# Gate logits from un-normalised rows, the last rows normalised by ACT, and the first expert's slots loaded in two halves

## The reference

```
h = layernorm(x) * (1 + ca) + sa
x = x + ga * attention(h)                # 16 heads of 16, causal
h = layernorm(x) * (1 + cb) + sb
logits = h @ gate_weight.T               # 8 experts
probs = softmax(logits); top = argmax(logits)
rank of a token = how many earlier tokens chose the same expert; kept if rank < 320
y = probs[top] * gelu(h @ wi[top]) @ wo[top]      # kept tokens only, exact gelu
x = x + gb * y
```

## Time and profile before

| what | value |
|---|---|
| runs | 784.5, 790.14, 792.09 us |
| median | 790.14 us |
| span of the profiled execution | 782.6 us |
| time of the profiled execution | not given apart from its span |
| PE busy | 689.1 us, 88% |
| DVE busy | 561.1 us, 72% |
| ACT busy | 459.5 us, 59% |
| POOL busy | 133.9 us, 17% |
| mean granted clock of TensorE | 0.943 |
| DMA | 66.53 MB, 85 GB/s over the span |

### The profile page before, as it was taken

How to read it: one execution, slowest core, us unless ns; L and a number is a source line. 1 busy time by engine, 2 the same in 40 slices (tenths; PEclk the granted TensorE clock), 3 DMA queues, 4 the chain that set the end, 5 groups by cost and what they waited for, 6 DMA issues and landing times.

```text
span 782.6 us, 12208 instructions
## 1 busy us (share of the span) xinstructions
PE 689.1 (88%) x4290; PEld 367.2 (47%) x4290; DVE 561.1 (72%) x1467; ACT 459.5 (59%) x962; POOL 133.9 (17%) x194
## 2 busy tenths in 40 slices
PE   4686989999999998999999999989996279999994
PEld 3564534432323343323332323242543269999994
DVE  7754778788888787988888898960435437777762
ACT  1422445566676667766677676657783336656551
POOL 6000222220001132003310201100105300121122
PEclk9869889999999999999999999999999559999998
DMA  7436126630006033005900006000004283455200
GB/s 243 109 76 144 41 57 147 162 68 14 2 0 162 1 81 81 2 1 124 308 1 1 1 1 214 1 28 1 28 28 162 90 234 115 155 182 201 92 23 17
DMA packets 42111, 66.53 MB, mean 85 GB/s; under 512 B 3822, under 2 KB 31985, under 8 KB 41466
## 3 DMA queue, kind: packets, MB, share of 16 engines
q1 hardware_dynamic: 39746, 59.44, 27.3%
q0 software_dynamic: 2304, 6.31, 2.2%
HBM read 39.36 MB, written 26.78 MB: 85 GB/s over the span
## 4 chain that ended last, share of the span: by engine, by line
PE 74%; DVE 10%; ACT 8%; issue 4%; DMA 2%; POOL 1%; SPq 0%; DVEq 0%; POOLq 0%; ACTq 0%
PE bank L1245 17%; PE bank L1295 15%; PE bank L1325 14%; PE bank L1430 9%; PE bank L1413 8%; ACT probs L802 4%; PE bank L1187 3%; DVE chunk_max L1049 2%; PE bank L1350 2%; PE bank L1216 1%; PE bank L1396 1%; ACT qk_sb L751 1%; PE bank L1373 1%; PE bank L1228 1%; DVE stats L907 1%
## 5 line engine op out<-in xcount | busy, mean ns | idle before, releaser
L802 ACT ACTIVATE probs<-bank 128x512 f32<-128x512 f32 (+3 forms) x640 | 298.3, 537 | 124.1 <-PE bank L1325 123.0
L1049 DVE TENSOR_REDUCE chunk_max<-bank 128x1 f32<-128x512 f32 x384 | 250.7, 685 | 36.9 <-PE bank L1295 35.9
L1325 PE MATMUL bank<-stacks 104*128 104x512 bf16 (+3 forms) x640 | 195.4, 356 | 13.5 <-ACT probs L802 10.1
L1295 PE MATMUL bank<-stacks 96*128 96x512 bf16 (+3 forms) x640 | 197.7, 359 | 7.9 <-DVE chunk_max L1049 3.2
L1245 PE MATMUL bank<-probs,v_sb 128*32 128x512 f32 (+3 forms) x1280 | 151.6, 546 | 0.1
L1055 DVE CUSTOM_DVE_ANT_0 masked<-bank,causal 128x128 bf16<-128x128 f32 (+3 forms) x256 | 120.7, 484 | 15.4 <-PE bank L1295 14.6
L1295 PEld LDWEIGHTS bank<-stacks 96*128 96x128 bf16 x640 | 56.0, 98 | 160.0 <-DVE chunk_max L1049 79.4
L698 POOL TENSOR_SCALAR_AFFINE_SELECT probs<-probs 128x512 f32<-128x512 f32 x64 | 40.6, 635 | 397.4 <-ACT probs L802 397.4
L1325 PEld LDWEIGHTS bank<-stacks 104*128 104x128 bf16 x640 | 62.2, 100 | 98.7 <-ACT probs L802 65.6
L1430 PE MATMUL bank<-w_split,acts 128*128 128x256 f32 x576 | 79.9, 284 | 0.0
L1430 PEld LDWEIGHTS bank<-w_split,acts 128*128 128x128 f32 x576 | 74.5, 190 | 1.5 <-issue 0.8
(11 more groups left out here) (140 smaller groups left out, 533.6 us busy)
## 6 DMA issues: line engine op xcount, KB each, us to landing
stacks<-qk_rows SPq DMA_DIRECT2D x6, 1536.0 KB, 12.4
w_raw<-w_in SPq DMA_DIRECT2D x8, 1024.0 KB, 5.0
w_raw<-w_down SPq DMA_DIRECT2D x8, 1024.0 KB, 8.0
qk_rows<-part SPq DMA_DIRECT2D x32, 192.0 KB, 2.9
slot_rows<-empty SPq DMA_DIRECT2D x1, 5140.0 KB, 28.9
slots_sb<-slot_rows SPq DMA_DIRECT2D x8, 514.0 KB, 4.0
qk_rows<-part SPq DMA_DIRECT2D x32, 128.0 KB, 2.4
stacks<-qk_rows SPq DMA_DIRECT2D x8, 384.0 KB, 4.5
```

Of the source, the lines that this page charges most:

```text
L802: act.activation(probs[:, s % 3, h, 0:width], bank[SCORE_BANKS[u % 3]][:, 0:width], ACT.Exp)\
L1049: dve.tensor_reduce(to, src[:, 0:QB], AX.X, ALU.max).then_inc(max_read, 1)
L1295: pe.matmul(bank[MAX_BANKS[u % 3]][:, 0:width], stack(g, 0)[0:KR, h, q0:q0 + P], stack(g, 1)[0:KR, h, c * QB:c * QB + width], start=True, ...
L1325: pe.matmul(bank[SCORE_BANKS[u % 3]][:, 0:QB - lo], stack(g, 1)[0:KR + MR, h, kt * P:(kt + 1) * P], stack(g, 0)[0:KR + MR, h, b * QB + lo: ...
```

## The change

The gate's logits are formed from the turned x1 itself. With r the inverse root of a row's variance and m its mean, the normalised row times the scaled gate weights w' is r * (x1 @ w' - m * sum(w')), and that is r * (x1 @ (w' - column mean of w')). So the weights are centred once, at `gate_bias`: a second product with the scale's column in `product[:, 1]` puts the column sums of w' into columns E to 2E of the bank, and DVE subtracts them, divided by D, from the weights. `choose` multiplies by `rstd` and then adds the bias. `turn_normal` transposes `x_sb` and waits for `x1_ready`; the semaphore `xhat2_ready` is gone. The first 12 tiles are still normalised by DVE, for the scatter alone; the last four by ACT, behind the gate's exponential, with -mean * rstd as bias; POOL waits for each of them before its scatter. Expert 0's slots are loaded in two halves: columns 256 to 513 first, columns 0 to 255 behind the slots of experts 1 to 3; DVE waits for the second half in `add_rows`.

```diff
-        xhat2T = rest[:, :].rearrange("p (r n) -> p r n", r=2)
+        x1T = rest[:, :].rearrange("p (r n) -> p r n", r=2)
...
-        def load_slots(eng, e):
-            rows = slot_rows[e * CAP:(e + 1) * CAP, :]
-            eng.dma_start(slots_sb[:, e % SR, 0:CT3 - 1, :],
+        def load_slots(eng, e, cols=slice(0, ROW), done=None):
+            done = done or slots_loaded[e % SR]
+            rows = slot_rows[e * CAP:(e + 1) * CAP, cols]
+            eng.dma_start(slots_sb[:, e % SR, 0:CT3 - 1, cols],
...
             sp.wait_ge(scattered, 16 * NT)
-            for e in range(SR):
+            load_slots(sp, 0, slice(D, ROW), slots_first)
+            for e in range(1, SR):
                 load_slots(sp, e)
+            load_slots(sp, 0, slice(0, D))
...
                     for t in range(t0, t1):
+                        if t >= TAIL_TILES:
+                            pool.wait_ge(last_normal, t - TAIL_TILES + 1)
                         pool.indirect_dma_start(
...
                     act.activation(expd[:, t0:t1, :], expd[:, t0:t1, :], ACT.Exp).then_inc(exp_gate, 1)
+                    if t1 == NT:
+                        act.wait_ge(rstd_ready, 1)
+                        for i, t in enumerate(range(TAIL_TILES, NT)):
+                            act.activation(heads[:, t, :], x_sb[:, t, :], ACT.Identity, bias=shift_back[:, i:i + 1],
+                                           scale=rstd[:, t:t + 1]).then_inc(last_normal, 1)
...
-                    inverse_root(slice(t + 1 - TB, t + 1))
-                    for i in range(t + 1 - TB, t + 1):
-                        dve.tensor_scalar(heads[:, i, :], x_sb[:, i, :], mean_var[:, i, 0:1], rstd[:, i:i + 1],
-                                          ALU.subtract, ALU.mult).then_inc(xhat2_ready, 1)
+                    ts = slice(t + 1 - TB, t + 1)
+                    inverse_root(ts)
+                    if t < TAIL_TILES:
+                        for i in range(t + 1 - TB, t + 1):
+                            dve.tensor_scalar(heads[:, i, :], x_sb[:, i, :], mean_var[:, i, 0:1], rstd[:, i:i + 1],
+                                              ALU.subtract, ALU.mult)
+                    else:
+                        dve.scalar_tensor_tensor(out=shift_back[:, :], in0=mean_var[:, ts, 0], scalar=-1.0,
+                                                 in1=rstd[:, ts], op0=ALU.mult, op1=ALU.mult).then_inc(rstd_ready, 1)
...
-                                  bias, ALU.add).then_inc(logits_read, 1)
+                                  wide(rstd[:, ts]), ALU.mult).then_inc(logits_read, 1)
                 dve.wait_ge(logits_read, part_no + 1)
+                link(dve.tensor_tensor(logits[:, ts, :], logits[:, ts, :], bias, ALU.add))
...
-                    for ft in range(DT):
-                        shift = dve.tensor_scalar(product[:, 0, ft * P:(ft + 1) * P], ones_f[:, :],
-                                                  mod_col[:, 2, ft:ft + 1], None, ALU.mult)
-                    shift.then_inc(gate_rows_ready, 1)
+                    for m in range(2):
+                        for ft in range(DT):
+                            rows = dve.tensor_scalar(product[:, m, ft * P:(ft + 1) * P], ones_f[:, :],
+                                                     mod_col[:, 2 + m, ft:ft + 1], None, ALU.mult)
+                    rows.then_inc(gate_rows_ready, 1)
                     dve.wait_ge(misc_done, misc_use[ev] + 1)
-                    dve.tensor_copy(gate_bias[:, :], bank[MISC_BANK][:, 0:E]).then_inc(misc_read_v, 1)
                     for ft in range(DT):
                         scaled = dve.tensor_scalar(w_gate_sb[:, ft, :], w_gate_sb[:, ft, :], mod_col[:, 3, ft:ft + 1],
                                                    None, ALU.mult)
-                    scaled.then_inc(w_gate_ready, 1)
+                    link(scaled)
+                    for ft in range(DT):
+                        centred = dve.scalar_tensor_tensor(out=w_gate_sb[:, ft, :], in0=bank[MISC_BANK][:, E:2 * E],
+                                                           scalar=-1.0 / D, in1=w_gate_sb[:, ft, :], op0=ALU.mult,
+                                                           op1=ALU.add)
+                    centred.then_inc(w_gate_ready, 1)
+                    dve.tensor_copy(gate_bias[:, :], bank[MISC_BANK][:, 0:E]).then_inc(misc_read_v, 1)
...
             def add_rows(e, st):
+                if e == 0:
+                    dve.wait_ge(slots_loaded[0], 32)
...
-                    for k in range(DT):
-                        mm = pe.matmul(bank[MISC_BANK][:, 0:E], product[:, 0, k * P:(k + 1) * P], w_gate_sb[:, k, :],
-                                       start=(k == 0), stop=(k == DT - 1))
+                    for m in range(2):
+                        for k in range(DT):
+                            mm = pe.matmul(bank[MISC_BANK][:, m * E:(m + 1) * E], product[:, m, k * P:(k + 1) * P],
+                                           w_gate_sb[:, k, :], start=(k == 0), stop=(k == DT - 1))
...
-                    emptied(xhat2T_ready, t)
-                    pe.wait_ge(xhat2_ready, t + 1)
+                    emptied(x1T_ready, t)
+                    pe.wait_ge(x1_ready, t + 1)
                     for ft in range(DT):
-                        mm = pe.transpose(bank[tail_bank(2, t)][:, ft * P:(ft + 1) * P], heads[:, t, ft * P:(ft + 1) * P],
+                        mm = pe.transpose(bank[tail_bank(2, t)][:, ft * P:(ft + 1) * P], x_sb[:, t, ft * P:(ft + 1) * P],
...
             def turn_slots(e):
-                pe.wait_ge(slots_loaded[e % SR], 32 * (e // SR + 1))
+                if e == 0:
+                    pe.wait_ge(slots_first, 32)
+                else:
+                    pe.wait_ge(slots_loaded[e % SR], 32 * (e // SR + 1))
```

More of the change, by code:

```diff
@@ L321, in layer @@
         rstd = sb("rstd", [P, NT], F32)
+        shift_back = sb("shift_back", [P, TB], F32)
         product = sb("product", [P, 2, D], F32)
@@ L451, in layer @@
         x1_ready = sem("x1_ready")
-        xhat2_ready = sem("xhat2_ready")
-        xhat2_turned = sem("xhat2_turned")
-        xhat2T_ready = sem("xhat2T_ready")
+        rstd_ready = sem("rstd_ready")
+        last_normal = sem("last_normal")
+        x1_turned = sem("x1_turned")
+        x1T_ready = sem("x1T_ready")
+        slots_first = sem("slots_first")
         gated = sem("gated")
@@ L519, in load_expert @@
                           w_down[e].rearrange("(t p) n -> p t n", p=P)).then_inc(w_loaded[e % 2], 16)
-        def load_slots(eng, e):
-            rows = slot_rows[e * CAP:(e + 1) * CAP, :]
-            eng.dma_start(slots_sb[:, e % SR, 0:CT3 - 1, :],
-                          rows[0:(CT3 - 1) * P, :].rearrange("(t p) d -> p t d", p=P)).then_inc(slots_loaded[e % SR], 16)
-            eng.dma_start(slots_sb[0:LAST_ROWS, e % SR, CT3 - 1, :],
-                          rows[(CT3 - 1) * P:CAP, :]).then_inc(slots_loaded[e % SR], 16)
+        def load_slots(eng, e, cols=slice(0, ROW), done=None):
+            done = done or slots_loaded[e % SR]
+            rows = slot_rows[e * CAP:(e + 1) * CAP, cols]
+            eng.dma_start(slots_sb[:, e % SR, 0:CT3 - 1, cols],
+                          rows[0:(CT3 - 1) * P, :].rearrange("(t p) d -> p t d", p=P)).then_inc(done, 16)
+            eng.dma_start(slots_sb[0:LAST_ROWS, e % SR, CT3 - 1, cols], rows[(CT3 - 1) * P:CAP, :]).then_inc(done, 16)
         def rows_of(st):
@@ L819, in _ @@
                     t = ev[1]
-                    act.wait_ge(xhat2_turned, t + 1)
+                    act.wait_ge(x1_turned, t + 1)
                     if t >= 2:
                         act.wait_ge(gated, t - 1)
-                    act.copy(xhat2T[:, t % 2, :], bank[tail_bank(2, t)][:, 0:D]).then_inc(xhat2T_ready, 1)
+                    act.copy(x1T[:, t % 2, :], bank[tail_bank(2, t)][:, 0:D]).then_inc(x1T_ready, 1)
                 if ev[0] == "gate_exp":
@@ L1357, in _ @@
                         pe.wait_ge(counts_read, 1)
-                    emptied(xhat2T_ready, t)
-                    pe.wait_ge(xhat2_ready, t + 1)
+                    emptied(x1T_ready, t)
+                    pe.wait_ge(x1_ready, t + 1)
                     for ft in range(DT):
-                        mm = pe.transpose(bank[tail_bank(2, t)][:, ft * P:(ft + 1) * P], heads[:, t, ft * P:(ft + 1) * P],
+                        mm = pe.transpose(bank[tail_bank(2, t)][:, ft * P:(ft + 1) * P], x_sb[:, t, ft * P:(ft + 1) * P],
                                           ident[:, :])
-                    mm.then_inc(xhat2_turned, 1)
+                    mm.then_inc(x1_turned, 1)
                 if ev[0] == "gate":
@@ L1370, in _ @@
                         pe.wait_ge(w_gate_ready, 1)
-                    pe.wait_ge(xhat2T_ready, t + 1)
+                    pe.wait_ge(x1T_ready, t + 1)
                     for k in range(DT):
-                        mm = pe.matmul(bank[MISC_BANK][:, t * E:(t + 1) * E], xhat2T[:, t % 2, k * P:(k + 1) * P],
```

(3 more changed lines are left out.)

## The result

Over 20 runs each, on one chip, the changed kernel took 778.38 us in the median (776.12 to 785.48) and the kernel before 783.64 (781.86 to 792.09). The ratio is 0.9921 with a 95% interval of 0.9897 to 0.9944, which is some 6.2 us; the medians lie 5.3 apart. Medians and ranges hold all runs, ratios leave out those over 1.5% above the fastest run of their kernel. I forecast 785.6, from 781.0 to 791.6, so the measured time lies outside the range, though its sign was forecast and 0.8% is within the 1% that I gave the highest chance. The profiled executions have spans of 782.6 and 774.4, 8.2 apart; that one of the changed kernel took 776.12 in all, 1.7 more than its span. It is the fastest of its 20 runs, so the 8.2 of the profiled pair is more than a usual execution gains.

The account below looks back on a forecast made before the run. It took a serial chain from 600.77 to 629.28 us, before the experts, and another around the gate's bias as bounding. Terms -5.8 + 0.2 + 0.1 + 0 - 1.0 + 1.7 + 0.3 = -4.5 took 790.14 to 785.6 us, range 781.0 to 791.6.

Parts of the forecast that it names:

- (a): Last four tiles: TensorE turns x1 instead of normalised rows, so the choice starts at 605.0 instead of 610.81, -5.8 us.
- (b): Last choice of experts on DVE: one more dependent instruction, multiply by rstd then add the bias, +0.2 us.
- (c): Last four rows normalised by ACT beside the choice: no cost; four more waits on POOL, +0.1 us.
- (d): Last four scatters, from destinations to SP's first slot load: the same 9.3 us, so 0, bounds -1.6 and +1.0.
- port rival: Scatters stretch beside every one of DVE's four differences, one more by 1.0: 786.6 us, chance 0.10.
- (e): Expert 0's slots, half the columns loaded first: TensorE starts sooner after SP's first issue, -1.0 us, bounds 0 and -1.5.
- (f): Gate's bias and centred weights near 75.6 us: extra products and DVE steps delay the first row maxima's turn, +1.7 us.
- (g): First choice, for twelve tiles: the same extra instruction while TensorE waits, +0.3 us, bounds 0 and 0.4.
- slower rival: Early attention: TensorE's longer idle brings two more half-clock dips of 6 us, +6: 791.6 us, chance 0.15.
- half-clock rival: Last gates run at half clock, ending at 606.2 after the root; (a) gains 4.6, not 5.8: 786.8 us, chance 0.05.

Follow-up runs that it names:

- after_third: The changed kernel run once more, unaltered, on the same chip as its variants: median 782.18 us, ratio 0.9921 to the kernel before.
- before_centred: The kernel before with only the new gate_bias event, the second product and the centring of the weights: ratio 0.9987 to the kernel before.
- keep_busy: The changed kernel plus 46 unread identity matmuls on TensorE, in five portions between the second count and expert 0's slots: ratio 0.993 to the kernel before.
- tail_busy: The changed kernel with gate bias later, DVE's expert 0 weight parts behind the scatters, and unread identity matmuls in six portions: ratio 0.984 to the kernel before.

## Why the forecast was wrong, by its own steps

**The level was the step that failed.** The forecast said "I put the difference on the median", 790.14, of three runs between 784.5 and 792.09, though the span of the profiled execution was 782.6 and the lowest run lay 1.9 above it. The sum had been made from that execution. 20 runs put the kernel before at 783.64, 6.5 lower, which is more than the whole effect. From there the same sum, -4.5, gives 779.1, 0.7 from the measured 778.38. The span alone would have done nearly as well: every run here takes 1.7 or 1.8 more than its span, and 782.6 + 1.8 - 4.5 is 779.9. The range was built from the costs alone and held nothing for the level, though the three runs already lay 7.6 apart. That the sum fits the medians so closely (-4.5 against -5.3) is in part luck, since several terms were off, as follows.

**(a)** was right in kind, the root last and the gates done 0.8 ahead, and in size in two of three executions of the changed kernel: -5.8 forecast, -5.9 measured. The third (after_third) has the output projection in part at half clock, took 12.44 instead of 10.76, and gains 4.2. **(b)** +0.2, measured +0.22. **(c)** nothing, as measured: ACT's four rows take 2.06 us beside the choice, with 1.2 to spare; the four waits on POOL cost nothing (steps of 0.30 as before), not 0.1.

**(d)** I kept 9.3 and got 8.83, 9.20 and 9.20 in three executions. The stretch is DVE's, as the port rival has it, but it did not grow: the first scatter now goes ahead of DVE's first part, and 1.3 of stretch is left of 1.6. That rival's "one more by 1.0" is refuted.

**(e)** was mis-sized: -1.0 forecast with a bound of -1.5, -1.7 to -1.9 measured in the experiments, in both kernels, and only -1.2 in after_third (3.89). I took the size from the landings of two other loads, and halving this one's rows saved more than they do; why was not taken apart.

**(f) and (g)**: +1.7 at the turned maxima, measured 1.67, and (f) alone left 1.4 at the last heads (before_centred). Together 2.0 forecast, 1.5 measured, which leaves about 0.1 for (g) instead of 0.3, by one execution against one. The delay travels nearly whole.

**Not in the sum**: where the clock comes back in the first expert, -1.3 in the profiled pair. The forecast had the row and put nothing on it. With (e) at its measured size it takes the sum from -4.5 to -6.6; the ratio says 6.2. The slower rival, two more dips in the early attention, did not happen: over the first 200 us the mean granted clock was 0.90 before and 0.91 after, with as many half-clock pieces. The clock does move the total by some 5 us from one execution to the next, in both kernels, and that does not tell them apart. The half-clock rival was wrong: the gates ran at full clock in all three executions, and what one of them had at half was the output projection ahead of them. Why the clock came back sooner behind the shorter idle, 10.0 to 10.7 us behind the first transpose in three executions of the changed kernel against 13.0, was not taken apart.

## What to carry to other kernels

Make the sum against the profiled execution and state the result as a difference; the level comes from many runs, and where three of them lie 1% apart the range has to hold that too. In a serial chain look for what needs only the raw value: the transposes and the product with the weights could go ahead of the statistics, and 5.9 us came of it. Then ask where the work that was added elsewhere stands in the order: the gate's bias cost 4.4 us at its first place (1.7 of it by what the change added), 5.5 in the second and 1 in the third.

## What the runs showed of the hardware that I had not expected

TensorE's clock was at half for 9.0, 6.2 or 6.8 us of the first expert, which cost 0.44 to 0.47 us for each. In keep_busy a piece with TensorE 79% idle for 2 us (636 to 638), behind a busy stretch, was followed by 6.8 us at half, and matmuls without use in that piece gave 3 us (tail_busy). Two executions of one program lay 4.9 us apart, 4.6 of it in four groups of matmuls at half clock. DVE's subtraction of two SBUF tiles stretched a scatter's issue on POOL from 0.97 to 1.97, and four such scatters by 1.3 in all. A load of 320 rows of 1032 bytes let TensorE start 3.0 to 3.9 us behind its issue over fourteen executions, one of 2056 bytes 4.8 to 5.1 behind it over three.
